# A graph-network layer on one core: the gather engine's second group of every round waits for a later matmul

## The reference

```
h   = relu(layernorm(x));  s = h[:, :64];  v = h[:, 64:] as (n, 32, 3)
xs  = s @ W1_s / 8;        xv = v @ W1_v / sqrt(32)        # per node
w   = silu(emb @ fc_w1 + fc_b1) @ fc_w2 + fc_b2            # per edge, 192 values
msg = w * (xs, xv)[src] * sh, in four combinations         # per edge, 96 + 288 values
agg = segment_sum(msg, dst)
out = x + h + gate(agg @ W2 + h @ Wsc)                     # gate: silu
```

## Time and profile before

| | us |
|---|---|
| median of 3 runs | 737.73 |
| lowest and highest run | 734.68, 742.15 |
| the profiled execution | 733.41 |
| its span, first to last instruction | 731.7 |
| mean granted TensorE clock | 0.755 of full speed |

### The profile page before, as it was taken

One profiled execution on the slowest core, in us unless ns is written; L12 is line 12 of the kernel. 1 busy time (PEld: TensorE's weight loads), 2 busy tenths in 40 slices (PEclk: granted clock), 3 DMA queues, 4 the chain that ended last, 5 costly groups with the idle time before them and its releaser, 6 DMA issues.

```text
span 731.7 us, 16598 instructions
## 1 busy us (share of the span) xinstructions
PE 560.1 (77%) x4599; PEld 393.1 (54%) x4599; DVE 425.4 (58%) x1406; ACT 220.8 (30%) x448; POOL 389.8 (53%) x417
## 2 busy tenths in 40 slices
PE   3866679779767777776877797779889787877766
PEld 3744445546554655554555465545656555554545
DVE  4675566448466645736654674655665575455745
ACT  2563232223223222322322332222232233233131
POOL 7364555455555555645546555555645546355540
PEclk8887677587889767868866777785667778678777
DMA  9441122122222222212222222222212222121110
GB/s 231 115 120 45 48 55 57 49 60 49 59 58 53 55 57 53 58 48 55 60 53 63 53 54 53 54 54 58 52 45 56 57 55 55 44 57 48 51 43 21
DMA packets 35834, 44.11 MB, mean 60 GB/s; under 512 B 10490, under 2 KB 28254, under 8 KB 35783
## 3 DMA queue, kind: packets, MB, share of 16 engines
q0 software_dynamic: 19392, 33.12, 18.3%
q1 hardware_dynamic: 14957, 10.07, 5.5%
q10 hardware_dynamic: 1434, 0.40, 0.3%
HBM read 39.56 MB, written 4.00 MB: 60 GB/s over the span
## 4 chain that ended last, share of the span: by engine, by line
SPq 62%; issue 28%; PE 5%; DVE 2%; DMA 1%; ACT 1%; another core or an unknown queue 0%; DVEq 0%
SPq L549 41%; SPq L552 18%; SPq L541 2%; PE ps L446 1%; PE ps L980 1%; PE ps L447 1%; DMA x_sb<-x 1%; PE ps L437 1%; SPq L546 1%; PE ps L931 0%; PE ps L436 0%; PE ps L921 0%; PE ps L944 0%; ACT hT L267 0%; DVE z_sb L331 0%
## 5 line engine op out<-in xcount | busy, mean ns | idle before, releaser
L595 POOL DMA_INDIRECT gath<-table,src_sb x380 | 364.9, 960 | 305.5 <-PE ps L944 111.7
L944 PE MATMUL ps<-fc_sb,hid 128*128 128x384 f32 x416 | 208.8, 636 | 3.7 <-issue 3.7
L949 PEld LDWEIGHTS ps<-S,P 128*64 128x64 f32 x832 | 96.4, 160 | 124.8 <-issue 102.3
L949 PE MATMUL ps<-S,P 128*64 128x12 f32 x832 | 118.8, 222 | 52.2 <-issue 28.7
L950 PE MATMUL ps<-S,P 128*64 128x12 f32 x832 | 119.7, 223 | 33.1 <-issue 33.1
L808 DVE TENSOR_TENSOR agg<-ps,agg 128x48 f32 x412 | 84.5, 205 | 88.1 <-ACT res L621 52.5
L951 PE MATMUL ps<-S,P 128*64 128x36 f32 x832 | 123.0, 246 | 12.3 <-issue 12.3
L952 PE MATMUL ps<-S,P 128*64 128x36 f32 x832 | 123.4, 247 | 10.1 <-issue 10.0
L944 PEld LDWEIGHTS ps<-fc_sb,hid 128*128 128x128 f32 x416 | 100.2, 252 | 54.8 <-issue 33.4
L730 DVE TENSOR_TENSOR S<-iota,dstrel 128x48 f32<-128x48 f32 x104 | 25.2, 242 | 170.6 <-remote 158.9
L950 PEld LDWEIGHTS ps<-S,P 128*64 128x64 f32 x832 | 97.2, 160 | 39.1 <-issue 39.1
(11 more groups left out here) (127 smaller groups left out, 560.5 us busy)
## 6 DMA issues: line engine op xcount, KB each, us to landing
slow<-table SPq DMA_DIRECT2D x901, 0.6 KB
slow<-table ACTq DMA_DIRECT2D x512, 0.6 KB
gath<-table,src_sb POOLq DMA_INDIRECT x380, 2.5
out<-res SPq DMA_DIRECT2D x24, 78.1 KB
x_sb<-x SPq DMA_DIRECT2D x5, 350.0 KB
emb<-emb_t SPq DMA_DIRECT2D x52, 32.0 KB
table<-prod SPq DMA_DIRECT2D x3, 420.0 KB
sh_sb<-sh_t SPq DMA_DIRECT2D x1, 840.0 KB
```

The costliest lines, as they stand in the source:

```text
L595: nc.gpsimd.indirect_dma_start(gath[:, u, j, :], None, table, bass.IndirectOffsetOnAxis(ap=src_sb[:, t:t + 1], axis=0)).then_inc(arrived, 16)
L944: ins = nc.tensor.matmul(w_ps(u)[:, 2 * g:2 * g + 2, 0:WN], hid[:, u % 2, g, :], fc2_sb[:, :, :], start=False, stop=True, skip_group_check ...
L949: nc.tensor.matmul(oj[0:64, :, 0], pj[:, 0:64], sj[:, :, 1], start=True, stop=True)
```

## The change

In front of the gathers of every group with u = 1 (from round 1 on) POOL waits until the weights of group q - 1, the group directly in front (u = 0), are done, instead of those of group q - 2. The groups with u = 0, 2 and 3 wait as before. No instruction is added or removed.

```diff
--- before.py
+++ after.py
@@ -586,7 +586,7 @@
                         u = q % SLOTS
                         if q >= SLOTS:
                             pool.wait_ge(p_prod, q - SLOTS + 1)
-                            pool.wait_ge(p_w, q - 1)
+                            pool.wait_ge(p_w, q if u == 1 else q - 1)
                         raw_tile = u == SLOTS - 1 and q // SLOTS >= RAW_FROM
                         slow_tile = u == 1 and q // SLOTS >= SLOW_FROM or u == 2 and q // SLOTS >= ACT_FROM
                         for j in range(QT - raw_tile - slow_tile):
```

## The result

The changed kernel took 803.12 us (median of 4 runs, 796.51 to 811.19), the kernel before 736.2 beside it: ratio 1.089, 95% interval 1.083 to 1.095. So it is 67 us slower, 2.6 us a round; forecast were 751, with a range of 725 to 774. The traced execution of the changed kernel was the slowest of its four (811.19 us), so its span is 77.7 us above that of the kernel before, and what is counted in the two traces has to be held against 77.7, not 67.

What follows compares the result with a forecast made beforehand. Bound: a loop of POOL's gather bursts and PE signals held until each drains. Rounds of 18.06 + 1.8 + 3.6 + 2.9 = 26.4 us against 25.64 gave 13 us more in total: 751, range 725 to 774.

Steps and rivals of the forecast that it cites:

- burst, release of PE's signal, next burst: POOL and PE: PE's signals wait until a gather burst drains; a round is 18.06 us issuing and 7.58 waiting.
- The bursts and the three other waits: POOL: bursts of 4, 8 and 3 gathers; waits of 1.8 us ahead of slot 0, 0.30 slot 2, 2.9 slot 3.
- The gates: ACT, L620: they start 1 to 2.3 us after slot 2's last gather, with more idle time in one piece.
- The wait ahead of slot 1: POOL: a new wait for `weights` of slot 0, some 1.8 to 5.5 us, taken as 3.6.
- The sum: Whole kernel: 0.7 to 0.8 us more a round, 9 us over rounds 5 to 16, 4 in 13 others, 13 total.
- What is gained meanwhile: DVE at L730: its 5.3 us wait goes; ACT's gates and DVE's first add of slot 1 wait for the moved burst.
- The cover of the gathers: Slot 1's gathers: 9 us in hand before DVE uses them, moved by 7.7 us at most, so cover holds, barely.
- Much slower: PE at its lower clock every round: new wait 5.5 us, round 28.3, time 777 us; chance 0.10.
- Faster: PE keeps the higher clock through `weights` of slot 0: new wait 1.8 us, round 24.6, time 722; chance 0.20.
- The argument on queues that take turns: DMA engines: software and hardware queues take turns, so gathers would not starve fetches and nothing would depend on bursts.
- no change: SP's queue sets the round and hides POOL's order: 738 us; chance of a time within 1%, 0.25.
- The Trainium skill's rule: Slot 1's gathers: a later start can only lose; by it the sum is 0 while the 9 us in hand last.

Runs made afterwards that it cites:

- n1: The kernel before without the row fetches of SP and ACT: 702.49 us against 738.28 for the kernel before in the same job, ratio 0.954.
- k4: The kernel before with no wait for `weights` ahead of any group: 545.47 us against 546.24 for the kernel before, ratio 1.000.
- n3: The kernel before with no wait for `weights` ahead of any group, fetches kept: 837.77 us against 738.28 for the kernel before, ratio 1.139.
- n2: The changed kernel without the row fetches of SP and ACT: 773.64 us against 738.28 for the kernel before, ratio 1.052.
- h1: The kernel before without the row fetches of SP and ACT: 533.08 us against 547.65 for the kernel before, ratio 0.974.
- m1: The kernel before with every row fetch of SP issued twice: 956.8 us against 735.87 for the kernel before, ratio 1.301.
- k2: The kernel before with the later wait ahead of slot 0 instead of slot 1: 552.79 us against 546.24, ratio 1.012.

## Why the prediction was wrong

**What bounds the kernel.** Right in kind: the loop "burst, release of PE's signal, next burst" is there, and SP's queue was a bystander (2% of the chain after, and 36 us in all for its fetches in n1). Wrong in one part: the reading gave the hold to gathers together with fetches. n1 has no fetches and shows it all the same.

**The bursts and the three other waits.** Right: 4, 8, 3; 1.31, 0.31 and 2.50 us against 1.8, 0.3 and 2.9. The gates come 1.8 us after the last gather of the burst of eight (419.52 against 417.70), as forecast.

**The wait ahead of slot 1.** This is the step that failed, with "`weights` of slot 0 ends 6.4, 5.6, 9.4 us after the round's first gather" as its basis. 3.6 us were taken, the middle between 1.8 and 5.5; in rounds 5 to 16 it is 7.0 (7.2 over rounds 4 to 18), above both ends. A small part was there to be read: the middle of two rows stood in for a mean, and the mean of the kernel before in these rounds is 8.2 us, which by the same sum (less 4.7, plus 0.8) gives 4.3. The greater part came with the change: `weights` of slot 0 now end 11.0 us after the round's first gather. In round 12, the scatter ahead of them runs into slot 0's burst and is held (4.1 us for 1.2), and then the rest runs with the granted clock at 0.50 (5.1 for 2.8); the table of rounds 4 to 18 shows the same in all but two. I took a duration that depends on the order of the bursts from the old order and moved it into the new one. Why PE comes to slot 0's burst in a worse place than before I can only argue: the burst of eight lies two waits earlier, and PE has its arrears behind it.

**The sum.** Forecast 0.7 to 0.8 us a round; waits sum to 3.3 more, the period to 3.5. In the traces rounds 5 to 16 cost 41 us (forecast 9) and the rest of the kernel 36 (forecast 4, as the 13 other rounds were taken at 0.3).

**What is gained meanwhile.** Right in kind. DVE's wait ahead of L730 in slot 0 did go: 4.7 us on average in rounds 4 to 18 before, 0.0 after (404.52 in round 12). But others came in its place, in slot 1 behind the burst of eight (3.5 us on average, 5.94 at 414.57) and in slot 3 (2.7, 2.44 at 400.36), which the prediction didn't have, and L730 has 183.9 us of idle time in all against 170.6.

```profile
400.36 0.24 DVE L730 TENSOR_TENSOR S<-iota,dstrel 128x48 f32<-128x48 f32 x1 [2.44 <-remote]
404.52 0.24 DVE L730 TENSOR_TENSOR S<-iota,dstrel 128x48 f32<-128x48 f32 x1
...
414.57 0.24 DVE L730 TENSOR_TENSOR S<-iota,dstrel 128x48 f32<-128x48 f32 x1 [5.94 <-remote]
```

ACT's gates, late behind the burst of eight as forecast, hold DVE's first add of slot 1 up longer. The page, before and after:

```profile
L808 DVE TENSOR_TENSOR agg<-ps,agg 128x48 f32 x412 | 84.5, 205 | 88.1 <-ACT res L621 52.5
L808 DVE TENSOR_TENSOR agg<-ps,agg 128x48 f32 x412 | 84.5, 205 | 137.1 <-ACT res L621 98.3
```

**The cover of the gathers** held but for 5.4 us of the whole kernel.

**The rivals.** "Much slower" had half of the mechanism (the lower clock in every round) and stopped at 777, since its wait ended at 5.5; PE's held instructions were not in it, though the earlier trace rows showed PE standing still. "Faster" falls, in the 547 jobs too. The argument on queues that take turns, set beside "no change", decides nothing here: n1 has no fetch to take turns with, and its signals come late all the same. The Trainium skill's rule in "DMA: Bandwidth & Descriptors", Rules for kernel authors (issue early, wait late) has the right sign for this change. But k4 and n3, which follow it further than the kernel before, gain nothing at 547 and lose 14% at 736; there the measurement goes against it.

**What is shown and what is not.** Shown: the loss needs no fetch (n1, n2); it is there whenever `weights` of slot 0 stand ahead of slot 1 (24, 23, 71, 67, 76 us in five pairs); in 736 jobs about half of PE's signals come late, and the holes in PE's scatter grow by 66, 55 and 74 us where the traces grow by 78, 65 and 75; in the measured kernel holes and low clock stand ahead of the late `weights` in 13 of 15 rounds; in 547 jobs neither late signals nor holes exist and 23 us remain, a plain dependence on a POOL that never rests. Only argued: that the holes cause the low clock and the late `weights`. No run takes the holes away in a 736 job and leaves the rest, and in n2 they stand elsewhere for the same loss. Open: why the same program meets held signals in one job and none in another; I could not choose, and no run set it off or stopped it. A version that beats the kernel before was not found.

## What to carry to other kernels

A wait that carries no data may still be load-bearing: before moving it, ask which pause it makes, and who uses that pause. When a change reorders bursts, a duration read inside the old order is no bound for the new one; follow the late engine's whole queue from the last point where it was in step. And where a result rests on idle time "remote" or "issue", measure more than once before explaining it: here the change cost 4% or 9% by the job alone.

## What the runs showed of the hardware that was not expected

- While POOL issued indirect gathers (0.95 us each, 0.30 apart), PE's semaphore signals could be counted late in 736 jobs, in the burst shown 1.5 us after its last gather: 105 of 190 later than 0.7 us with no row fetches running (n1), 0 of 221 in a 547 job (h1).
- In the 736 jobs PE's own instructions stopped for up to 2.6 us, above all inside the scatter with its many small matmuls: 47 (m1) to 165 us (n3) a kernel, 0 in the 547 jobs (one of 0.2 us in k2). SP's register moves stopped too, for up to 1.48 us.
- The same kernel took 547 or 736 us. The gathers' own issue was the same in both (951 and 960 ns on average).
- A memset of 128 x 2048 f32 on POOL took 1.83 us.
